# Two-layer transformer kernel: layer norm by ScalarE two ticks ahead, expert numbers in PSUM, whole QKV blocks in layer 2, expert bias as a two-row product

## The reference

```
x = x + 0.5 * dora_ffn(ln(x))     # W + B A, each column scaled
x = x + attention0(ln(x))         # 32 query heads, 8 key heads, dim 16, rotary, causal
x = x + 0.5 * dora_ffn(ln(x))
x = x + 0.5 * moe(ln(x))          # x W^T + b_base, plus 2 of 8 rank-16 experts
x = x + attention1(ln(x))         # 8 heads of dim 32
x = x + 0.5 * moe(ln(x))
# moe: top-2 of 8 router logits -> softmax of the two -> gate w[t, e]
#      lora_out = sum_e w[t,e] * 2.0 * (x A_e^T) B_e^T
```

## Time and profile before

| | us |
|---|---|
| median of 3 runs (lowest, highest) | 1398.65 (1390.51, 1400.39) |
| the profiled execution, as timed | 1391.04 |
| its span, first to last instruction | 1389.3 |
| PE busy in the span | 1220.1 (88%) |
| DVE busy | 1017.3 (73%) |
| ACT busy | 573.0 (41%) |
| POOL busy | 412.5 (30%) |

### The profile page before, as it was taken

How to read it: one execution, slowest core, us unless ns; L and a number is a source line. 1 busy time by engine, 2 the same in 40 slices (tenths; PEclk the granted TensorE clock), 3 DMA queues, 4 the chain that set the end, 5 groups by cost and what they waited for, 6 DMA issues and landing times.

```text
span 1389.3 us, 21472 instructions
## 1 busy us (share of the span) xinstructions
PE 1220.1 (88%) x6800; PEld 753.2 (54%) x6800; DVE 1017.3 (73%) x2894; ACT 573.0 (41%) x827; POOL 412.5 (30%) x601
## 2 busy tenths in 40 slices
PE   3888999999898878997868989999988987889877
PEld 1675444443377765444756744444435776744367
DVE  5778899997168967744858888999852798686266
ACT  1221576665622252553212126666655223435421
POOL 1531231121265400216415413122214562002262
PEclk9996699998899997999989958999999999979999
DMA  8346211220010022000040742112200100120001
GB/s 308 114 129 152 93 42 32 55 63 2 1 48 1 1 46 70 1 2 25 37 169 0 207 110 81 25 25 55 63 2 1 48 0 16 31 70 2 1 9 54
DMA packets 37283, 76.19 MB, mean 55 GB/s; under 512 B 5084, under 2 KB 6620, under 8 KB 37036
## 3 DMA queue, kind: packets, MB, share of 16 engines
q1 hardware_dynamic: 37176, 74.82, 18.6%
HBM read 48.98 MB, written 27.08 MB: 55 GB/s over the span
## 4 chain that ended last, share of the span: by engine, by line
PE 62%; DVE 25%; issue 5%; ACT 4%; DMA 2%; SPq 1%; POOL 1%; DVEq 0%; ACTq 0%; POOLq 0%
PE bank L986 16%; PE bank L860 12%; PE bank L768 5%; PE bank L970 4%; DVE maxes L1208 4%; PE bank L770 4%; PE bank L769 4%; PE bank L964 3%; PE bank L754 3%; DVE probs L1044 3%; DVE unused L1204 2%; DVE ops L1147 2%; PE bank L870 2%; DVE stats L1029 2%; DVE gate L1089 2%
## 5 line engine op out<-in xcount | busy, mean ns | idle before, releaser
L1407 ACT ACTIVATE probs<-bank 128x1024 f32<-128x1024 f32 (+3 forms) x416 | 368.1, 911 | 333.1 <-PE bank L970 226.2
L860 PE MATMUL bank<-ops 48*128 48x512 f32 (+3 forms) x960 | 320.0, 439 | 22.8 <-DVE maxes L1204 8.1
L1204 DVE CUSTOM_DVE_ANT_0 unused<-bank,causal 128x128 bf16<-128x128 f32 (+3 forms) x640 | 279.6, 485 | 39.6 <-PE bank L860 36.0
L1522 POOL TENSOR_SCALAR_AFFINE_SELECT probs<-probs 128x256 f32<-128x256 f32 (+1 forms) x256 | 118.8, 464 | 635.3 <-ACT probs L1407 635.1
L860 PEld LDWEIGHTS bank<-ops 48*128 48x128 f32 (+1 forms) x960 | 162.8, 207 | 205.7 <-DVE maxes L1204 84.1
L986 PE MATMUL bank<-probs,v_mem 128*17 128x512 f32 (+6 forms) x1920 | 255.5, 524 | 6.1 <-ACT heads_raw L1394 5.6
L1208 DVE TENSOR_REDUCE maxes<-bank 128x1 f32<-128x512 f32 x320 | 207.0, 683 | 41.0 <-PE bank L860 39.6
L970 PE MATMUL bank<-ops 50*128 50x512 f32 (+2 forms) x640 | 176.7, 452 | 9.1 <-DMA ops<-shiftT 4.8
L1315 ACT CAST xT<-bank 128x512 fp32r<-128x512 f32 (+1 forms) x96 | 52.5, 551 | 232.0 <-PE bank L754 232.0
L768 PE MATMUL bank<-ops,xT 128*128 128x512 f32 (+1 forms) x288 | 116.4, 404 | 24.6 <-DVE x L1064 19.0
L970 PEld LDWEIGHTS bank<-ops 50*128 50x128 f32 x640 | 87.5, 199 | 66.3 <-issue 34.7
(11 more groups left out here) (114 smaller groups left out, 2012.3 us busy)
## 6 DMA issues: line engine op xcount, KB each, us to landing
query_rows_dram<-ops SPq DMA_DIRECT2D x48, 256.0 KB, 3.5
ops<-query_rows_dram SPq DMA_DIRECT2D x64, 192.0 KB, 4.2
w_odd<-staging_wqkv SPq DMA_DIRECT2D x4, 1536.0 KB, 6.7
x<-x_dram SPq DMA_DIRECT2D x16, 256.0 KB, 6.0
ops<-ops SPq DMA_DIRECT2D x16, 256.0 KB, 3.0
out_dram<-x SPq DMA_DIRECT2D x16, 256.0 KB, 2.0
staging_wqkv<-wqkv_dram SPq DMA_DIRECT2D x2, 1536.0 KB, 16.1
key_rows_dram<-ops SPq DMA_DIRECT2D x24, 128.0 KB
```

The source lines that it names most:

```text
L860: last = mm(dst[:, h * w:(h + 1) * w], queries(a, u)[rows, t // 4, hi, t % 4 * P:(t % 4 + 1) * P], keys(a, u, hi)[rows, HALF * kp:HALF * k ...
L1204: V.tensor_tensor_reduce(unused[:, masked % 3, 0:w], part, causal[:, HALF - w:], 1.0, NEG, ALU.add, ALU.max, dst).then_inc(s["max_done"].s ...
L1407: A.activation(probs[:, e % 6, :, 0:cols], scores[:, 2 * (e % 2):2 * (e % 2) + 2, 0:cols], ACT.Exp, scale=a.scale).then_inc(s["exp"].sem, 1)
L1522: G.affine_select(out=p, in_=p, compare_op=ALU.is_ge, fill=0.0, base=0, pattern=pattern, channel_multiplier=-1).then_inc(s["masked"].sem, 1)
```

## The change

Seven edits.

1. `normalise` moves from DVE to ACT, as rstd * x + (-mean * rstd), two ticks ahead, with six `xn` buffers in place of two. DVE's `statistics` now also writes var + eps and -mean (two operations on 128x1), and runs three ticks ahead; POOL keeps only the power.
2. `turned_lo` comes before the epilogue in a DVE tick, and the epilogue of an expert tile one tick later instead of two. PE turns n-1 before the first half of tile n and adds its lora inside the first half.
3. ACT copies `expert_no` into PSUM at the start of chains 1 and 2, and `weigh` reads it there.
4. The expert bias leaves POOL: PE adds it to each half as a product of two rows of ones by a high and a low row of the bias.
5. In layer 2, ACT and DVE write a block's high and low part in one operation each to a staging buffer in `features`; SP stores three pieces to DRAM and loads the operands (`standard_operands`), as layer 1 does.
6. In chain 0 the second group of value products moves ahead of the last four query blocks, and the ring items are spread between the chunks of the products: in the last four ticks 28 items instead of 12 in chain 0, 14 instead of 12 in chain 1.
7. The QKV0 turns begin one tick later (three ticks with two turns instead of four).

The core of the diff:

```diff
-            order = [(0, 0), (1, 0), (2, 0), first, (0, 1), (1, 1), (2, 1), (3, 0), (4, 0), (3, 1), (4, 1), second]
-            self.begun = {8: 3, 9: 6, 10: 9, 11: 12}
+            order = [(0, 0), (1, 0), (2, 0), first, (0, 1), (1, 1), (2, 1), second, (3, 0), (4, 0), (3, 1), (4, 1)]
+            self.ring_in = {8: (1, 1, 2, 2), 9: (1, 1, 2, 2), 10: (2, 2, 2, 2), 11: (2, 2, 2, 2)}
         else:
             order = [(0, 0), (1, 0), first, (3, 0), (0, 1), (1, 1), (3, 1), second, (2, 1), (2, 0)]
-            self.begun = {5: 2, 6: 4, 7: 6, 8: 9, 9: 12}
+            self.ring_in = {5: (0, 0, 1, 1), 6: (1, 1, 1, 1), 8: (0, 0, 1, 1), 9: (1, 1, 2, 2)}
...
-        early = len(plain) - (3 if chain[-2] in MOE_RANK else 4)
+        early = len(plain) - 3
...
+            def standard_operands(b):
+                a, s = A1, qs[QKV1]
+                for n, (j, g) in enumerate(blocks1):
+                    rows = (k1_rows if j % 2 else q1_rows)[4 * (j // 2):4 * (j // 2) + 4].rearrange(
+                        "h (p d) s -> p h d s", p=3)[:, :, :, HALF * g:HALF * (g + 1)]
+                    hi, lo = (m.bitcast(F32) for m in high_low(n))
+                    sp.wait_ge(s["hi"].sem, s["hi"].at(b, n + 1))
+                    sp.dma_start(rows[0], hi).then_inc(block_stored[n].sem, 16)
+                    sp.dma_start(rows[1 if j % 2 else 2], hi).then_inc(block_stored[n].sem, 16)
+                    sp.wait_ge(s["read"].sem, s["read"].at(b, a.product_no("qk", j, g) + 1))
+                    sp.dma_start(rows[2 if j % 2 else 1], lo).then_inc(block_stored[n].sem, 16)
+                    if n % 2 == 1:
+                        load_standard(b, n - 1)
+                        load_standard(b, n)
+
+            def load_standard(b, n):
+                j, g = blocks1[n]
+                half = slice(HALF * g, HALF * (g + 1))
+                sp.wait_ge(block_stored[n].sem, block_stored[n].at(b, 48))
...
             def expert_half(b, st, t, first, between=None):
...
+                dst = prod[n % 2][:, 1 if first else 0, 0:MOE_HALF]
+                mm(dst, two_ones[:, :], base_pair[:, cols], start=True, stop=False)
+                last = three_passes(dst, n, weights(st, 0)[:, :, cols],
+                                    weights(st, 1)[:, :, cols], lora=not first, between=between, begun=True)
...
+                    if before is not None:
+                        turn_hw(b, *before)
                     if tick.product is not None and tick.product[0] in MOE_RANK:
-                        expert_half(b, *tick.product, True)
-                        if before is not None:
-                            turn_hw(b, *before)
-                        expert_half(b, *tick.product, False, between=lora_between)
+                        expert_half(b, *tick.product, True, between=lora_between)
+                        expert_half(b, *tick.product, False)
...
+                V.tensor_scalar(var_eps[:, n % STAT_SLOTS, :], mv[:, n % STAT_SLOTS, 1:2], EPS, None, ALU.add
+                                ).then_inc(ln_eps.sem, 1)
+                V.tensor_scalar(minus_mean[:, n % STAT_SLOTS, :], mv[:, n % STAT_SLOTS, 0:1], -1.0, None, ALU.mult
+                                ).then_inc(ln_minus.sem, 1)
...
-                V.tensor_scalar(gate[:, 1, :], expert_no[:], top_atf[:, 1:2], route[:, 0:1], ALU.is_equal, ALU.mult
+                V.tensor_scalar(gate[:, 1, :], numbers, top_atf[:, 1:2], route[:, 0:1], ALU.is_equal, ALU.mult
...
-                    for h in range(4):
-                        hi, lo = head_rows1(j, h, g)
-                        last = V.scalar_tensor_tensor(lo, src[32 * h:32 * (h + 1), :], bias_head1[:, 4 * j + h:4 * j + h + 1],
-                                                      hi.bitcast(F32), ALU.add, ALU.subtract)
-                    last.then_inc(s["read"].sem, 1)
+                    V.scalar_tensor_tensor(lo, src, bias_qk1[:, j:j + 1], hi.bitcast(F32), ALU.add, ALU.subtract
+                                           ).then_inc(s["read"].sem, 1)
...
+                A.mul(ln_bias[:, i, :], minus_mean[:, i, :], rstd[:, i, :]).then_inc(ln_scaled.sem, 1)
+                act.wait_ge(ln_scaled.sem, ln_scaled.at(b, n + 1))
...
+                A.activation(xn[n % XN_SLOTS], x[:, t, :], ACT.Identity, bias=ln_bias[:, i, :], scale=rstd[:, i, :]
+                             ).then_inc(xn_ready.sem, 1)
```

268 lines of the change are left out of this document (137 added, 131 removed).

## The result

The changed kernel takes 1485.34 us (median of 4 runs, 1481.65 to 1486.21) against 1396.16 us of the kernel before, a ratio of 1.064 (95% interval 1.059 to 1.068): 89 us slower, where 20 us faster was forecast and the range ended at 1410 us. Its profiled execution has a span of 1483.1 us, 93.8 more than that of before.

What follows compares the result with a forecast made beforehand. TensorE was taken to bound the kernel, with short scattered waits to remove. A -23, B -21, C +19.5 and D +5 gave about -20 us, from 1398.65 to 1378 us; range 1346 to 1410 us.

Steps and rivals of the forecast that it cites:

- D: QKV1 up to attention 1's first score: DVE and ACT save, DRAM stores and loads cost more; +2.4 us, both times +5.
- B: Expert ticks (MOE_A, MOE_B): shorter loop without slow gate operations, bias products at 0.15 us each; -21 us.
- C: End of QKV0 to attention 0's first score: last product behind more ring items, later shifts; +9.5 us per sequence, +19.5 in all.
- first rival: Starts of both attentions: shifts behind more transfers, TensorE at 1.2 GHz; slower, near 1411 us; chance 0.20.
- sum of the four delays: Sign deciding for the first rival: the delays of the four first attention scores add to over 44 us.
- A: Norm moved ahead onto ACT: shorter waits in FFN_A, QKV0 and WO1; -23 us.
- third rival: Expert ticks: something else closes the loop or 128x1 operations block behind POOL, no gain there; near 1400 us; chance 0.15.
- second rival: Round trips through DRAM hide, C +10 and D -20; faster, near 1345 us; chance 0.20.

Runs made afterwards that it cites:

- e1: The changed kernel with layer 2's rows in DRAM as 3 x 128 x 1024, so stores write 128 rows and each load becomes three; 1397.81 us (1.004).
- e9: The changed kernel with its own layout and loads, each layer 2 store split into four, one per head; 1433.91 us (1.027).
- e3: The changed kernel with chain 0's product order and ring items as before; 1456.35 us (1.043).
- e7: e1 with 12 ring items, three after each of the last four products, instead of 28, new product order kept; 1375.24 us (0.987).
- e12: The kernel before with one edit alone, the gate reading the expert numbers in PSUM; 1368.42 us (0.984).
- e10: The changed kernel with the mends of e1, e3 and e4 together, and the gate reading the expert numbers in SBUF again; 1396.87 us (0.999).
- e4: The changed kernel with POOL adding the expert bias again and no bias products on TensorE; 1461.09 us (1.047).
- e6: Mends of e1, e3 and e4 together, with attention 0's first shift rows loaded ahead of units 1 and 2's queries and WO0's weights; 1347.81 us (0.965).
- e11: e6 with attention 1's first shift rows also loaded ahead of the last 12 query loads and WO1's and MOE_B's weights; 1333.23 us (0.958).

## Why the prediction was wrong

Forecast and measurement are 113 us apart (-19.5 and +93.8 in the profiled executions). By the rows of the table, 73 us of that are D's stretch, 18 the expert stages (B), 9 the stretch of C, 9 attention 0, and the rest small.

**The step that failed: D, the price of a store.** D took "some 0.9 us each of the 16 engines" for stores and loads alike, from layer 1's rows, and put the round trips at +5 us, with +30 as the bound "if they don't keep up". It measured +78.1. The rows were layer 1's, for stores of 16 x 8 rows; the changed kernel's are of 4 x 32 rows and go at 102 GB/s on a share of 0.26, by which the three of a block (786 KB) take 7.7 us where I had 2.7. e1, which spreads them (and splits the loads), brings the stretch to 65.6 and 65.3 us, +1.7 and +1.5 over before, where D had said +2.4, and its first score comes 17.3 us after the last product, where D had said 18. e9 keeps the layout and shows that the shape of the store alone makes 51 us of the kernel's time. The bound was wrong for the same reason as the value: it allowed for waiting, not for another rate. D's own rows could have warned: 12.6 MB at the 189 GB/s that it quotes are 67 us, more than the stage of 63.7 us, and not the "some 50" of its sum. The first rival was on the right side, and the sum of the four delays "over 44 us" from which it decides was reached twice over (102 us), but its mechanism, TensorE's clock and the number of transfers, was not the one.

**C was right in its cause and too low.** It priced the ring ahead of the last product at +9.5 us for each sequence. By e3, which undoes that part alone, it costs 12.3 and 15.3 us, and by e1 against e7 14 and 11; the table's +9.3 and +14.5 are a net of C and of what the other edits give in the same stretch. From SP's first store of the second keys to the first score it is 31.9 us before and 44.9 in the changed kernel (96.94 and 86.85 are the stores), +13. The 42 us that C gave for it are not worked out from its rows: 3 and 3.0 for the store, 5.0, 10 and 14.00 are 35. e7 shows that the product order has no part in it. The place was only half right: TensorE's wait for DMA in the ring is 2.4 us there in the first sequence, less than the 5 us I had put at the twelfth item; more is DVE's pace in reading and the low clock behind it (0.87 in the window, 0.92 in e7's). In the first sequence SP's shifts also wait for the bias row that edit 4 makes (DVE's three operations and one load, 121.29 to 124.53 us on the chain), for which C had 0.5 us.

**A's stretches came out a little high.** FFN_A lost 6.4 and 8.1 us (forecast 6 each), WO1 1.7 each (forecast 3), and QKV0 3.0 and 0.8 by e3 (forecast 2.6 each). The norm waits went as the rows of after show, from 50.1 to 15.9 us. Nothing came late on ACT: its norm takes 816 ns and the small product 296 ns, for 0.62 and 0.2 us in the sum, and TensorE waits for neither in the chains. Edits 1, 2 and 7 were never undone one by one, so that these gains belong to the three together: every kernel that has them takes 62.0 to 64.0 and 38.7 to 40.4 us up to the end of FFN_A, and the two without them 68.6 to 69.3 and 47.7 to 47.9.

**B was right in what was wrong before, and wrong in the sum.** The gate was what held the loop: e12 gives 7.3, 10.4, 7.5 and 5.2 us in the four stages by that edit alone, 30 us, and e10 takes 41 us of the same stages away again. The forecast of -21 us came to -3.0, because the bias products were mis-sized: "2 x 0.15" per tile, from DVE's smallest operation and from the turns of 128x128. 0.15 us is indeed what a pass of 324 columns and 128 rows takes from start to start. The product with two rows takes 0.35 us, and starts 0.09 to 0.15 us later behind its predecessor than a pass does; so it was no short pass, and the prediction's argument that a product's contents don't change its length did not cover it. In B's loop the product stands once, some 4 us over four stages; e4 shows 19.2 us. e4's stages, 47.2 and 41.5 us, are under what B forecast with a bias product of 0.15 us (49.6 and 45.7 in windows 0.5 and 3.2 us wider than the stages). B also took the first sequence's 52.40 us of MOE_B for both, where the second stage was 44.0 us and had little to give.

**The third rival** (DVE's 128x1 operations behind POOL) did not occur: 154 and 144 ns on average over 96 each, also in e4 where POOL is busier. What the Trainium skill says of the shared pair ("SBUF — State Buffer", section "SBUF: two separate sides") agrees with the gate: with the numbers in PSUM its operations don't wait.

**Attention 0** had no place in the forecast and gave +9.2 us, 8.0 of them in the first sequence. Over all profiled executions it takes 245.0 to 255.2 us in the first sequence and 246.6 to 254.2 in the second, with the same instructions in it but for e6's and e11's order of loads. So the 8 us are within the scatter and are not shown to come from the change; where they stand, the granted clock is lower (0.77 from 163 to 183 us of the changed kernel, 0.97 from 160 to 180 us of before).

**The range.** It ran from 1346 to 1410 us and was said to take in the second rival's centre and most of the first, but by the sums these centres are 1345 and 1411, both just outside. It did not decide anything here.

What stays open: what of C belongs to DVE's pace and what to the lower clock, since no run separates them; and what edits 1, 2 and 7 are worth one by one. The next step that the traces suggest is e11 with the second half's shift rows moved up as well.
